# Scores stage of a fused decoder block: x transposed from memory, its normalization as two spread lines on GpSimd

## What is computed

```python
def _layernorm(x, axis=-1, eps=1e-05):
    m = jnp.mean(x, axis=axis, keepdims=True)
    v = jnp.var(x, axis=axis, keepdims=True)
    return (x - m) / jnp.sqrt(v + eps)
# first attention; x is layernorm(x), k and v are the context
Q = jnp.einsum('bshd,hde->bshe', xh, Wh)
K = jnp.einsum('bshd,hde->bshe', kh, Wh)
V = jnp.einsum('bshd,hde->bshe', vh, Wh)
scores = jnp.einsum('bshe,bthe->bhst', Q, K) / jnp.sqrt(jnp.float32(hd))
masked = scores * Dn[None, :, :, :]
A = jnp.maximum(jnp.abs(masked.sum(axis=0)), 1.0)
O = jnp.einsum('hst,bthe->bshe', A, V).reshape(b, s, dim)
W = jax.nn.relu(x @ wg_w)
return W * Y @ wo_w            # Y: O, normalized over the row
```

## Time and profile before

| | |
|---|---|
| median of 3 runs | 2060.79 us (2059.82 to 2062.56) |
| the profiled execution | 2059.62 us, span of its trace 2057.8 us |
| PE busy | 1949.0 us, 95% of the span |
| PE weight loads | 1576.9 us |
| DVE busy | 1481.8 us, 72% |
| ACT busy | 1007.7 us, 49% |
| POOL busy | 1035.8 us, 50% |
| mean granted clock of TensorE | 0.975 of full speed |

### The profile page before, as it was taken

One profiled execution on the slowest core, in us unless ns is written; L12 is line 12 of the kernel. 1 busy time (PEld: TensorE's weight loads), 2 busy tenths in 40 slices (PEclk: granted clock), 3 DMA queues, 4 the chain that ended last, 5 costly groups with the idle time before them and its releaser, 6 DMA issues.

```text
span 2057.8 us, 27834 instructions
## 1 busy us (share of the span) xinstructions
PE 1949.0 (95%) x10162; PEld 1576.9 (77%) x10162; DVE 1481.8 (72%) x2201; ACT 1007.7 (49%) x1412; POOL 1035.8 (50%) x789
## 2 busy tenths in 40 slices
PE   7999869999997669999999999999999999999998
PEld 6789745666653658888888888888888888888786
DVE  6676658888884777867876876886886787687422
ACT  4336547777764445336337327335434633633532
POOL 1110144544430856665566655666565565566454
PEclk9999989999999779999999999999999999999999
DMA  5766424566645204224144233242332423422422
GB/s 205 283 225 240 154 82 119 148 158 162 166 109 131 65 29 133 88 85 152 62 118 136 71 112 111 97 116 84 122 108 82 139 73 108 144 78 67 133 93 67
DMA packets 170116, 249.74 MB, mean 121 GB/s; under 512 B 91356, under 2 KB 92764, under 8 KB 163708
## 3 DMA queue, kind: packets, MB, share of 16 engines
q1 hardware_dynamic: 169692, 247.86, 38.9%
q10 hardware_dynamic: 288, 0.10, 0.0%
HBM read 193.13 MB, written 33.69 MB: 110 GB/s over the span
## 4 chain that ended last, share of the span: by engine, by line
PE 63%; POOL 2%; issue 1%; DVE 1%; DVEq 0%; ACT 0%; POOLq 0%; ACTq 0%
PE e_ps_out L54 6%; PE e_ps_out L55 6%; PE e_ps_out L56 6%; PE e_ps_u L54 6%; PE e_ps_u L56 6%; PE e_ps_u L55 6%; PE e_ps_g L54 4%; PE e_ps_g L56 4%; PE e_ps_g L55 4%; PE e_ps_m L55 4%; PE e_ps_m L56 4%; PE e_ps_m L54 4%; PE e_ps_m L2843 1%; PE e_ps_m L2797 1%; PE e_ps_m L2833 1%
## 5 line engine op out<-in xcount | busy, mean ns | idle before, releaser
L1388 POOL TENSOR_TENSOR e_gu_lo<-e_gu_raw,e_gu_hi 128x1024 fp32r<-128x1024 f32 (+1 forms) x128 | 288.7, 2259 | 183.7 <-ACT e_gu_hi L1692 183.6
L2247 DVE TENSOR_REDUCE e_x3T<-e_zp 128x128 f32<-128x1024 f32 x124 | 258.4, 2084 | 6.4 <-ACT x_held L1807 5.3
L1393 POOL TENSOR_TENSOR e_dn_lo<-e_dn_raw,e_dn_hi 128x512 fp32r<-128x512 f32 x128 | 179.1, 1401 | 114.9 <-ACT e_dn_hi L1698 114.0
L54 PE MATMUL e_ps_u<-e_xn_hi,e_gu_hi 128*128 128x512 f32 x512 | 205.4, 401 | 0.0
L54 PE MATMUL e_ps_out<-e_hd_hi,e_dn_hi 128*128 128x512 f32 x512 | 204.1, 399 | 0.0
L56 PE MATMUL e_ps_u<-e_xn_hi,e_gu_lo 128*128 128x512 f32 x512 | 202.2, 395 | 0.0
L55 PE MATMUL e_ps_u<-e_xn_lo,e_gu_hi 128*128 128x512 f32 x512 | 202.2, 395 | 0.0
L55 PE MATMUL e_ps_out<-e_hd_lo,e_dn_hi 128*128 128x512 f32 x512 | 202.0, 395 | 0.0
L56 PE MATMUL e_ps_out<-e_hd_hi,e_dn_lo 128*128 128x512 f32 x512 | 202.0, 394 | 0.0
L2179 DVE TENSOR_TENSOR e_hd_lo<-gate_held,e_hd_hi 128x512 fp32r<-128x512 f32 x128 | 146.6, 1146 | 68.1 <-ACT e_hd_hi L1722 67.9
L1400 POOL TENSOR_TENSOR gate_held<-e_sg,e_wb 128x512 f32<-128x512 f32 x96 | 137.3, 1430 | 113.4 <-ACT e_sg L1706 72.0
(11 more groups left out here) (311 smaller groups left out, 5108.2 us busy)
## 6 DMA issues: line engine op xcount, KB each, us to landing
e_gu_raw<-in_mgu SPq DMA_DIRECT2D x96, 512.0 KB, 3.8
e_dn_raw<-in_md SPq DMA_DIRECT2D x128, 256.0 KB, 2.8
e_wb<-wts SPq DMA_DIRECT2D x8, 1536.0 KB, 7.7
c<-in_ctxT SPq DMA_DIRECT2D x8, 1024.0 KB, 6.5
raw_w<-in_w1T SPq DMA_DIRECT2D x8, 1024.0 KB, 4.9
x_held<-in_w2T SPq DMA_DIRECT2D x8, 1024.0 KB, 7.3
gates<-gate_held SPq DMA_DIRECT2D x8, 1024.0 KB, 4.9
vals<-o SPq DMA_DIRECT2D x8, 1024.0 KB, 4.3
```

The lines of the kernel that those rows point to most:

```text
L54: nc.tensor.matmul(out, w_hi, x_hi, start=first, stop=False, skip_group_check=skip)
L1388: nc.gpsimd.tensor_tensor(gu_lo[:, s % 2, a], gu_raw[:, s % 2, a], f32(gu_hi[:, s % 2, a]), ALU.subtract).then_inc(gulo_done, 1)
L1393: nc.gpsimd.tensor_tensor(dn_lo[:, s % 2], dn_raw[:, s % 2], f32(dn_hi[:, s % 2]), ALU.subtract).then_inc(dnlo_done, 1)
L2247: nc.vector.tensor_reduce(x3T[:, lb].rearrange("p (b n) -> p b n", b=B)[:, :, hh * CD:(hh + 1) * CD], zv(5, (1, 8), (21, 8)), AX.X, ALU.ad ...
```

## The change

Chunk 0 is made as before. For chunks 1 to 7 the host gives x a second time, transposed (`xT`), and no transposes are made in the kernel. The transposed x has its rows along the free dimension, so scale and shift, one number per row of x, must be the same in all partitions. VectorE and GpSimd compute them as before, four rows' numbers per partition (`own_lines`). SyncE stores them to memory as two lines of 512 numbers (write_lines) and loads the lines back into all 128 partitions (spread_lines). GpSimd multiplies the four parts of the transposed x by the first line and adds the second (normed, eight instructions), in place. ScalarE and VectorE cut the result from SBUF. The transposed x lies in the buffer of the normalized one, so it is loaded when the cuts of the chunk before are done (load_xT). x itself is now free for the next load as soon as its statistics are done.

In SyncE's round the store and the load of the lines stand behind the weight loads and ahead of the context. The loads of mask and gamma go from the beginning to the place behind round 5. The matmuls that clear the four score accumulators stand ahead of the transposes of chunk 0 instead of behind queries(0). They no longer have a buffer of zeros of their own, but use half of q_lo. The bf16 copy of the identity is gone, and some semaphores with one use are merged into others.

The core of the diff:

```diff
+        def load_xT(n):
+            sp.wait_ge(xnT_done, 4 * n)
+            sp.dma_start(xT, xT_v[n]).then_inc(xT_in, 16)
+        def write_lines(n):
+            sp.wait_ge(shift_done, n + 1)
+            sp.dma_start(dram["lines"][n].rearrange("a (j p) -> p a j", p=P), line[:],
+                         allow_slow_non_contiguous=True).then_inc(lines_out, 16)
+        def spread_lines(n):
+            sp.wait_ge(lines_out, 16 * n)
+            if n > 1:
+                sp.wait_ge(line_step, 8 * (n - 1))
+            sp.dma_start(lines[:], dram["lines"][n].unsqueeze(0).broadcast_to((P, 2, CH))).then_inc(lines_in, 16)
...
         def round_(i, part, load_weights, more_c, more_x):
             load_weights(part)
             if more_c:
+                write_lines(i + 1)
+                spread_lines(i + 1)
                 load_c(i + 1)
             sp.wait_ge(gate_done, 4 * (i + 1))
             sp.dma_start(dram["gates"][i], gate[:]).then_inc(gate_out, 16)
...
             sp.dma_start(dram["vals"][i], val[:]).then_inc(val_out, 16)
+            if more_x:
+                load_xT(i + 2)
...
         load_c(0)
         load_x(1)
+        load_xT(1)
...
-        sp.dma_start(keep["mask"][:], dram["mask"]).then_inc(const_in, 16)
-        sp.dma_start(keep["gam"][:], dram["gam"]).then_inc(const_in, 16)
...
         for i in range(HALF - 2):
             round_(i + HALF, i, load_w_round, True, True)
+        sp.dma_start(keep["mask"][:], dram["mask"]).then_inc(const_in, 16)
+        sp.dma_start(keep["gam"][:], dram["gam"]).then_inc(const_in, 16)
         round_(NCH - 2, HALF - 2, load_w_round, True, False)
...
+        def normed(n):
+            pool.wait_ge(xT_in, 16 * n)
+            pool.wait_ge(lines_in, 16 * n)
+            for k in range(KT):
+                nc.gpsimd.tensor_tensor(xT[:, k], xT[:, k], lines[:, 0], ALU.mult).then_inc(line_step, 1)
+            for k in range(KT):
+                pool.wait_ge(line_step, 8 * (n - 1) + k + 1)
+                nc.gpsimd.tensor_tensor(xT[:, k], xT[:, k], lines[:, 1], ALU.add).then_inc(line_step, 1)
         for i in range(1, NCH):
             power(i)
+            normed(i)
...
         def cut_x(n):
+            act.wait_ge(filled, filling(n - 1, QUERY + HEADS - 1))
             for k in range(KT):
-                act.wait_ge(filled, 16 * n + k + 1)
-                nc.scalar.activation(xnT_hi[:, k], bank[k][:], ACT.Copy).then_inc(xhi_done, 1)
+                act.wait_ge(line_step, 8 * (n - 1) + KT + k + 1)
+                nc.scalar.activation(xnT_hi[:, k], xT[:, k], ACT.Copy).then_inc(xhi_done, 1)
...
                 dve.wait_ge(xhi_done, 4 * n + k + 1)
-                nc.vector.tensor_tensor(xnT_lo[:, k], bank[k][:], f32(xnT_hi[:, k]), ALU.subtract).then_inc(xnT_done, 1)
+                nc.vector.tensor_tensor(xnT_lo[:, k], xT[:, k], f32(xnT_hi[:, k]), ALU.subtract).then_inc(xnT_done, 1)
...
         pe.wait_ge(small_in, 32)
-        turn(0, first=True)
+        clear_scores()
+        turn()
...
             gates(i)
             queries(i)
-            if i == 0:
-                clear_scores()
             if i < NCH - 1:
                 values(i)
-                turn(i + 1)
                 scores(i)
```

More of the change, by code:

```diff
@@ L83, in scores_block @@
     xn = sb("xn", [P, TJ, D])
+    xT = xn[:].rearrange("p (k a) n -> p k (a n)", k=KT)
+    lines = sb("held_lines", [P, 2, CH])
     xnT_hi, xnT_lo = (keep[n][:].rearrange("p a t d -> p (a t) d") for n in ("v_hi", "v_lo"))
@@ L96, in scores_block @@
     mom = sb("mom", [P, 5, TJ])
-    ve, rstd, shift, mhalf = (sb(n, [P, TJ]) for n in ("ve", "rstd", "shift", "mhalf"))
+    ve, mhalf, line = sb("ve", [P, TJ]), sb("mhalf", [P, TJ]), sb("own_lines", [P, 2, TJ])
+    rstd, shift = line[:, 0], line[:, 1]
     wpart, wsum, wrec = (sb(n, [P, 2]) for n in ("wpart", "wsum", "wrec"))
@@ L124, in filling @@
     def filling(i, use):
-        return 4 + 16 * i + use + 1
+        return 4 + 12 * i + use + 1
     block = st.enter_context(nc.Block())
@@ L132, in load_x @@
         def load_x(n):
-            sp.wait_ge(xn_done, START + 4 * n)
+            if n == 1:
+                sp.wait_ge(xn_done, 4)
+            elif n > 1:
+                sp.wait_ge(stats_done, 4 * n)
             if n == 0:
@@ L183, in _ @@
             round_(i + HALF, i, load_w_round, True, True)
+        sp.dma_start(keep["mask"][:], dram["mask"]).then_inc(const_in, 16)
+        sp.dma_start(keep["gam"][:], dram["gam"]).then_inc(const_in, 16)
         round_(NCH - 2, HALF - 2, load_w_round, True, False)
-        sp.wait_ge(xn_done, START + 4 * NCH)
-        sp.dma_start(keep["stage"][:], dram["vals"][0]).then_inc(v0_in, 16)
+        sp.wait_ge(stats_done, 4 * NCH)
+        sp.dma_start(keep["stage"][:], dram["vals"][0]).then_inc(x_in, 16)
         round_(NCH - 1, HALF - 1, load_w_round, False, False)
@@ L191, in _ @@
     def _(pool):
-        for t, value in ((mhalf[:], -0.5), (f32(zeros[:]), 0.0), (ones[:], 1.0), (wsum[:], 0.0), (rnd[:], ROUND), (unrnd[:], -ROUND)):
+        for t, value in ((mhalf[:], -0.5), (f32(zeros), 0.0), (ones[:], 1.0), (wsum[:], 0.0), (rnd[:], ROUND), (unrnd[:], -ROUND)):
             nc.gpsimd.memset(t, value).then_inc(consts_done, 1)
@@ L195, in power @@
             pool.wait_ge(mom_done, 6 * i + 6)
-            nc.gpsimd.tensor_tensor(rstd[:], ve[:], mhalf[:], ALU.pow).then_inc(rstd_done, 1)
+            if i == 1:
+                pool.wait_ge(xn_done, 4)
+            elif i > 1:
+                pool.wait_ge(lines_out, 16 * (i - 1))
+            nc.gpsimd.tensor_tensor(rstd, ve[:], mhalf[:], ALU.pow).then_inc(rstd_done, 1)
         pool.wait_ge(consts_done, 1)
@@ L245, in read_values, with norm @@
                 nc.scalar.activation(val[:, j], bank[j][:], ACT.Copy).then_inc(val_done, 1)
-        def norm(n):
-            act.wait_ge(shift_done, n + 1)
+        def norm():
+            act.wait_ge(shift_done, 1)
             for j in range(TJ):
@@ L278, in ternary @@
                 nc.scalar.activation(w_out[n][:, part], raw[n][:], ACT.Identity, bias=unrnd[:]).then_inc(tern_done, 1)
-        for s in (xn_done, tern_done):
-            act.sem_inc(s, START)
+        act.sem_inc(tern_done, START)
         act.dma_start(keep["ident"][:], dram["ident"]).then_inc(small_in, 16)
@@ L297, in round_ @@
                 cut_g()
-            norm(n)
             cut_q(i)
@@ L340, in norm_shift @@
             dve.wait_ge(rstd_done, n + 1)
-            nc.vector.scalar_tensor_tensor(out=shift[:], in0=mom[:, 0], scalar=-0.5, in1=rstd[:], op0=ALU.mult,
+            if n > 1:
+                dve.wait_ge(lines_out, 16 * (n - 1))
+            nc.vector.scalar_tensor_tensor(out=shift, in0=mom[:, 0], scalar=-0.5, in1=rstd, op0=ALU.mult,
                                            op1=ALU.mult).then_inc(shift_done, 1)
@@ L464, in _, with turn @@
     def _(pe):
-        def turn(n, first=False):
-            pe.wait_ge(xn_done, START + 4 * (n + 1))
+        def turn():
+            pe.wait_ge(xn_done, 4)
             for k in range(KT):
-                if not first:
-                    pe.wait_ge(val_done, START + 4 * (n - 1) + k + 1)
                 for j in range(TJ):
@@ L485, in clear_scores @@
             for h in range(HEADS):
-                nc.tensor.matmul(acc[:, h], zeros[:, 0:P], zeros[:], start=True, stop=False, skip_group_check=True)
+                nc.tensor.matmul(acc[:, h], zeros[:, 0:P], zeros, start=True, stop=False, skip_group_check=True)
         pe.wait_ge(small_in, 32)
-        turn(0, first=True)
+        clear_scores()
+        turn()
         pe.wait_ge(wglo_done, KT)
@@ L496, in gates @@
                     square_heads()
+                if i > 0:
+                    pe.wait_ge(val_done, START + 4 * (i - 1) + m + 1)
                 for k in range(KT):
@@ L588, in attn_block @@
      y_done, yg_done, qs_done, round_done, yq_done, h_done, gelu_done,
-     hs_done, hround_done, hq_done, mm2_done, x2_done, x2_out, early_in, consts_done, dq2w_done, shift_done) = (sem(n) for n in (
+     hs_done, hround_done, hq_done, mm2_done, x2_done, x2_out, early_in, consts_done, shift_done) = (sem(n) for n in (
          "v_in gate_in x_in vhi_done vlo_done o_done ostats_done omom_done orstd_done oshift_done on_done "
@@ L592, in attn_block @@
          "y_done yg_done qs_done round_done yq_done h_done gelu_done "
-         "hs_done hround_done hq_done mm2_done x2_done x2_out early_in consts_done dq2w_done shift_done").split())
+         "hs_done hround_done hq_done mm2_done x2_done x2_out early_in consts_done shift_done").split())
     keep["x2_out"] = x2_out
@@ L808, in _ @@
             act.sem_inc(s, START)
-        act.wait_ge(consts_done, 2)
+        act.wait_ge(consts_done, 3)
         for i in range(-3, NCH):
@@ L2745, in bias @@
             if g == 0:
-                pe.wait_ge(setup_lo, 2)
+                pe.wait_ge(setup_lo, 3)
                 pe.wait_ge(setup_hi, 2)
@@ L3205 @@
```

(1 more changed line is left out.)

55 lines of the change are left out of this document (28 added, 27 removed).

## The result

The changed kernel takes 2152.01 us (median of 4, 2151.1 to 2154.95) beside 2060.89 us for the kernel before on the same chip: a ratio of 1.0449, 95% interval 1.0434 to 1.0464, so 91 us slower. The forecast was 40 us more, 2101, and at most 2128.

The account below looks back on a forecast made before the run. TensorE bounded the kernel; afterwards a cut-to-cut loop of 30.85 us a round with sums would. Round 7 starting 37.4 us later plus about 2.5 us of half clock gave +40, 2101 us, range 2076 to 2128.

Parts of the forecast that it names:

- the loop: Cut to shift, store, spreading load, GpSimd, next cut in each scores round: 30.85 us with sums, against 26.45 before.
- What bounds the kernel, and what is removed: Scores rounds: TensorE bounds them; removing 16 transposes saves 1.69 us a round, leaving 24.75 us of TensorE work.
- (a): From the end of VectorE's cut to the next chunk's shift, unchanged: 11.05 us, 9.3 in clipping rounds.
- (d): GpSimd's eight instructions and the cut with it, alternation and wake-up included: 12.5 us, 11.5 to 14.2.
- (b): Store of the lines to memory, 1024 numbers of 4 bytes: 3.0 us, plus 0.15 for SyncE's issue.
- W: Time of the lines' store: taken as 3.0 us, at least 1.5, range's high end 5, at most 7.7.
- (c): Spreading load of 512 KB back into all partitions: 3.8 us to landing, 4.05 with SyncE's wait.
- S: Time of the spreading load: 4.05 us, low end 2.8, high end 5.
- Round 0: Chunk 1's lines go behind the weight loads, at 41.5 us, and its cut ends at 66.6; round 1 began at 49.4 before.
- The tail: Round 7, behind an idle TensorE: the first 7 us at half clock cost about 2.5 us that nothing hides.
- Other moves: Loads of context, gates, x, mask and gamma, and identity copy: mostly no cost; mask and gamma delay chunk 7's lines 2 us.
- the second one: Rival: the store of 4-byte pieces is the bound, W 7.7 us, +73 us, 2134 us; 12% chance.

Follow-up runs that it names:

- f_ahead: Changed kernel with lines stored in 256 pieces of 16 bytes and statistics, shift and store taken one chunk further ahead; 2053.35 us, 0.9970 of the kernel before.
- e_apart1: a_pieces16 plus a second store of the lines, 1024 pieces of 4 bytes side by side, which the spreading load also awaits; 2158.06 us.
- e_apart16: a_pieces16 plus a second store of 1024 pieces of 4 bytes in slots 64 bytes apart, which the spreading load also awaits; 2104.13 us.
- c_half: Changed kernel with two stores: scale line in 512 pieces of 4 bytes, shift line in 128 of 16 (wrong result); 2143.66 us.
- a_pieces16: Changed kernel with x loaded four neighbouring rows per partition, so lines are stored in 256 pieces of 16 bytes, not 1024 of 4; 2097.79 us.
- b_pieces32: Changed kernel with lines stored in 128 pieces of 32 bytes, one per partition, in another order (wrong result); 2089.04 us.
- d_store_first: Changed kernel with the lines' store ahead of the round's weight loads, and chunk 1's store and spreading load ahead of the wo wait; 2159.68 us.

## Why the prediction was wrong

The direction and the loop were right, and the size was not. By its own steps:

*What bounds the kernel, and what is removed*: right. Where the loop doesn't bind, a round takes 24.8 us (f_ahead), forecast 24.75. One slip: a round of 30.85 us leaves TensorE idle for 6.1 us and not for "some 5"; nothing was worked out from it.

*(a), 11.05 us from cut to shift*: 11.07. *(d), 12.5 us for GpSimd and the cuts*: 12.1, with GpSimd at 1.24 us an instruction in the multiplications and the alternation in the additions, at 1.46.

*(b), the store of the lines, W*: **this is the step that failed.** It put 3.0 us, with bounds of 1.5 and 5 for the range and 7.7 at the utmost. It measured 8.9 to 10.9 us in chunks 2 to 5, with at most 0.45 MB of weights still in front. The working doubled the nearest row, eight rows of 2 KB, for the number of the pieces. But the cost lies in 4-byte pieces packed without gaps (e_apart1 against e_apart16), not in their number (c_half), which no row of the kernel before could show, and the bound from above, a large load, had nothing to do with a store of this kind: I called it a bound because it was large. The seven gaps from store to spreading load sum to 78 us, while the prediction's terms sum to 34: 45 us too little.

*(c), S*, is the second term that was mis-sized: 4.15 to GpSimd's start; measured 4.3 to 6.6, together 9 us too little over seven chunks. Why the spreading load takes longer than the loads of its size was not looked into.

45 + 9, 1.6 for a later issue in round 0, less 3 for GpSimd's part, are 53 us. That is the distance between the forecast start of round 7, 255.3, and the measured one, 308.4. The loop carried every microsecond of it, once per chunk, into the time.

The check from the other side is a_pieces16. It has W at 1.6 to 2.7 us in the rounds with sums and, but for the way x is loaded, everything else as it was. Its cuts ended at 66.9, 97.8, 128.0, 158.3, 189.6, 221.1 and 253.0 us; the prediction's list for W = 3 is 66.6, 97.45, 128.3, 159.15, 190.85, 222.1 and 255.3. With that one term near its assumed size, the sum is right within 2.3 us after seven passes, and the whole is 2098 us against the 2101 forecast. That it comes out so close is partly luck: over the seven chunks the stores took 7 us less than the prediction's terms, the spreading loads 5 us more and GpSimd's part with the cut 2 us less. No other large error hides behind the first.

*Round 0*: the lines of chunk 1 were issued at 43.1 instead of 41.5, behind the weights as said. *The tail*: from the start of round 7 to the first product of the next stage it is 34.1 us against 31.8, at a mean granted clock of 0.85 instead of 0.94: 2.3 more, with 2.5 forecast.

*Other moves*: nothing of the context's load, the gates, the mask or the identity shows as a wait on the path.

*The rivals*: the second one named the right cause, the store of 4-byte pieces, and had 12%. Its price, 73 us, came from the bound of 7.7 and was too low for the same reason. It should have had a far larger share: it was the one operation of which the prediction itself said that no row shows it, it stood seven times in a loop that nothing hid, and I closed the range at W = 5 with a large part of the doubt outside. The Trainium skill (DMA: Bandwidth & Descriptors, Anatomy of one DMA) gives about 2.0 us of fixed cost for a transfer, fitted to transfers that GpSimd issues. The store of 16-byte pieces, which SyncE issues, lies near it, 1.6 to 2.7 us; the store of dense 4-byte pieces does not, and the measurement decides. The same page (Specifications) says that below 512 bytes a transfer is done by read-modify-write. No run shows the read, and both sizes lie below that mark, so the rule by itself does not tell the fast store from the slow one.

## What to carry to other kernels

Before a transfer is put between two engines, look whether what it feeds comes round again to what feeds it: in such a loop every link is paid once per pass, and its longest unknown link is the forecast's range. Store numbers that lie next to each other in memory from one partition, as a run, rather than as single numbers from many; here another assignment of rows to partitions was enough, and was worth 54 us. Issue nothing that is wanted soon behind a store of dense small pieces. And take what has a long latency one pass ahead, into a part of the program where nobody waits for it.

## What the runs showed of the hardware

A store of 1024 pieces of 4 bytes that fill 4 KB of memory without gaps is confirmed 8.9 to 10.9 us after its issue with little or nothing in front of it (chunks 2 to 5 of the changed kernel). Its packets are through in 1 to 2 us; the rest, 6.9 to 9.4 us, shows no traffic. In the same chunks it is 8.6 to 11.6 us with 512 such pieces (c_half), 1.6 to 2.7 with 256 pieces of 16 bytes (a_pieces16) and 1.4 to 2.4 with 128 of 32 bytes (b_pieces32). With each 4-byte piece in a slot of 64 or 512 bytes it is 3.5 to 4.3 (e_apart16, e_apart128). What happens in those microseconds, whether pieces from different DMA engines take turns on the same 64 bytes, no run shows. Slots of 8 to 32 bytes were not tried.

While such a store is unconfirmed, loads issued behind it hardly move: 38 GB/s in d_store_first, and 382 once it is confirmed. In f_ahead, where transfers stand behind a store of 16-byte pieces, the rate from 95.0 to 104.0 us was 340. The store itself took 9.8 to 12.4 us there.

VectorE's subtraction of two SBUF tensors and GpSimd's additions slow each other. Four subtractions take 2.49 us when GpSimd is done (f_ahead) and 5.19 beside its additions; the four additions took 5.82 us where the four multiplications took 4.95.
